# Two one-column shifts on the Vector engine written as one two-column instruction, in a cross-attention and feed-forward kernel

## The reference

```python
x = x + xattn(layernorm(x), ctx, ctx, igate_w, igate_b, fgate_w, fgate_b, out_w)   # 8 heads of 64
x = x + ffn(layernorm(x), kernel, input_scale, kernel_scale, bias)                 # fp8-rounded 512x512 product

def layernorm(x, eps=1e-05):
    m, v = mean(x), var(x)                 # over the 512 values of a row
    return (x - m) / sqrt(v + eps)
```

## Time and profile before

| What | us |
|---|---|
| median of 3 runs | 1698.84 |
| the runs | 1691.91, 1698.84, 1705.91 |
| the profiled execution, its own time | 1687.96 |
| its span, first to last instruction | 1686.2 |
| busy in it: PE, DVE, ACT, POOL | 1487.8, 1491.5, 1319.7, 1208.2 |

### The profile page before, as it was taken

One profiled execution on the slowest core, in us unless ns is written; L12 is line 12 of the kernel. 1 busy time (PEld: TensorE's weight loads), 2 busy tenths in 40 slices (PEclk: granted clock), 3 DMA queues, 4 the chain that ended last, 5 costly groups with the idle time before them and its releaser, 6 DMA issues.

```text
span 1686.2 us, 79011 instructions
## 1 busy us (share of the span) xinstructions
PE 1487.8 (88%) x31104; PEld 1046.6 (62%) x31104; DVE 1491.5 (88%) x4091; ACT 1319.7 (78%) x3206; POOL 1208.2 (72%) x1101
## 2 busy tenths in 40 slices
PE   1589998999999999899999899998999999999884
PEld 0366666666666666666666666666666666666662
DVE  5669999899989999989999899998999989998894
ACT  4568887888888888878888788887888878888662
POOL 2047777778777777867777777777777777777884
PEclk9789999999999999999999999999999999999996
DMA  5468888888888888877887878888788888887552
GB/s 182 135 197 250 261 257 246 247 250 257 260 242 267 253 257 245 265 239 241 261 251 257 251 238 253 264 254 257 245 250 260 263 251 245 270 253 233 192 170 82
DMA packets 138523, 402.61 MB, mean 239 GB/s; under 512 B 26216, under 2 KB 36456, under 8 KB 138152
## 3 DMA queue, kind: packets, MB, share of 16 engines
q1 hardware_dynamic: 138152, 397.52, 77.4%
HBM read 325.23 MB, written 72.22 MB: 236 GB/s over the span
## 4 chain that ended last, share of the span: by engine, by line
PE 31%; DVE 28%; DMA 19%; issue 13%; ACT 6%; POOL 3%; DVEq 1%; SPq 0%; ACTq 0%; POOLq 0%
DMA o_sb<-in_x 10%; PE work L555 7%; DMA out<-o_sb 5%; DVE o_sb L1076 5%; PE y L594 5%; DVE bn L1036 5%; DVE dec L982 4%; PE qk L523 4%; PE turn L451 4%; DMA x_sb<-in_x 3%; DVE bn L958 2%; PE turn L462 2%; POOL x L1234 2%; DVE carry L989 2%; DVE bn_h L1019 2%
## 5 line engine op out<-in xcount | busy, mean ns | idle before, releaser
L1216 POOL TENSOR_TENSOR x<-x,h_r 128x512 f32<-128x512 f32 x256 | 294.8, 1152 | 131.4 <-DVE x L1028 91.3
L1229 POOL TENSOR_TENSOR x<-x,w_out 128x512 f32<-128x512 f32 x256 | 358.1, 1399 | 17.7
L1234 POOL TENSOR_TENSOR x<-x,o_sb 128x512 f32<-128x512 f32 x256 | 321.4, 1277 | 52.9 <-DMA o_sb<-in_x 52.3
L555 PEld LDWEIGHTS work<-c_first,dec 128*64 128x64 f32 x4096 | 259.4, 138 | 93.6 <-issue 92.5
L555 PE MATMUL work<-c_first,dec 128*64 128x65 f32 x4096 | 291.1, 224 | 20.4 <-DVE carry L989 16.8
L555 PE MATMUL work<-c_sb,dec 128*64 128x65 f32 x4096 | 294.0, 225 | 0.0
L523 PE MATMUL qk<-qT,kT 64*64 64x128 f32 (+1 forms) x8192 | 238.5, 251 | 59.9 <-DVE dec L982 44.2
L594 PE MATMUL y<-w_ffn,zq 128*128 128x512 bf16 x1024 | 268.4, 385 | 2.2 <-issue 2.2
L523 PEld LDWEIGHTS qk<-qT,kT 64*64 64x64 f32 x8192 | 200.6, 134 | 100.4 <-issue 76.0
L555 PEld LDWEIGHTS work<-c_sb,dec 128*64 128x64 f32 x4096 | 259.2, 138 | 0.2 <-issue 0.2
L674 ACT ACTIVATE dec<-arg 128x384 f32<-128x384 f32 x512 | 243.0, 475 | 7.3 <-PE arg L505 6.1
(11 more groups left out here) (113 smaller groups left out, 3229.0 us busy)
## 6 DMA issues: line engine op xcount, KB each, us to landing
c_sb<-in_ctx SPq DMA_DIRECT2D x128, 520.0 KB, 7.2
x_sb<-in_x SPq DMA_DIRECT2D x128, 512.0 KB, 5.5
kT<-in_keys SPq DMA_DIRECT2D x128, 512.0 KB, 7.2
o_sb<-in_x SPq DMA_DIRECT2D x128, 512.0 KB, 5.2
out<-o_sb SPq DMA_DIRECT2D x128, 512.0 KB, 3.0
c_first<-in_ctx SPq DMA_DIRECT2D x256, 130.0 KB, 5.9
arg_queries<-query_parts SPq DMA_DIRECT2D x128, 144.0 KB
arg_keys<-key_parts SPq DMA_DIRECT2D x128, 12.0 KB
```

Of the source, the lines that this page charges most:

```text
L555: last = mm(work_ps[rows, u, c * W:(c + 1) * W], heads_dec[:, slot * Q:(slot + 1) * Q], src, start=True, stop=True)
L1216: pl.tensor_tensor(h, h, h_r[:, t * NH:(t + 1) * NH].unsqueeze(2).broadcast_to([P, NH, DH]), ALU.mult).then_inc(h_normed[t].sem, 1)
L1229: pl.tensor_tensor(h, h, w_out[:, :], ALU.mult).then_inc(h_scaled[t].sem, 1)
L1234: pl.tensor_tensor(x1[:, b.k % 2, t, :], x1[:, b.k % 2, t, :], o_sb[:, b.k % 2, t, :], ALU.add).then_inc(x1_set[t].sem, 1)
```

## The change

In `norm_scale` and in `mix_scale` the loop over the two tiles goes. It issued one tensor_scalar on one column each: the tensor input was the mean (mv, [128, 1]), the per-partition scalar operand was r ([128, 1]), and the second scalar the constant -1. In its place stands one scalar_tensor_tensor on two columns: (mv * -1.0) * r, with mv's two means (a stride of two elements) as first tensor and r's two columns as second tensor. The waits, the semaphore that is raised, and the place in DVE's order stay. Both tensors lie in SBUF.

```diff
@@ norm_scale
                 dve.wait_ge(*x_rstd.of(b))
                 if b.follows(2):
                     dve.wait_ge(*q_normed.of(b - 2))
-                for t in range(T):
-                    done = ts(nb1[:, b.k % 2, t:t + 1], mv1[:, b.k % 2, t, 0:1], r1[:, b.k % 2, t:t + 1], -1.0, ALU.mult, ALU.mult)
-                done.then_inc(x_shift.sem, 1)
+                stt(nb1[:, b.k % 2, :], mv1[:, b.k % 2, :, 0], -1.0, r1[:, b.k % 2, :], ALU.mult, ALU.mult).then_inc(x_shift.sem, 1)
@@ mix_scale
                 dve.wait_ge(*m_rstd.of(b))
                 if b.follows(1):
                     dve.wait_ge(*z_set.of(b - 1))
-                for t in range(T):
-                    done = ts(nb2[:, t:t + 1], mv2[:, t, 0:1], r2[:, t:t + 1], -1.0, ALU.mult, ALU.mult)
-                done.then_inc(m_shift.sem, 1)
+                stt(nb2[:, :], mv2[:, :, 0], -1.0, r2[:, :], ALU.mult, ALU.mult).then_inc(m_shift.sem, 1)
```

## The result

Measured: 1743.43 us median (1732.75 to 1753.44, 4 runs) against 1697.12 us of the kernel before with one more run, a ratio of 1.0267, 95% interval 1.0187 to 1.0346. The forecast was 1741 us. All ratios leave out executions over 1.5% above the fastest of their kernel; there is one, the profiled execution of e3 (1745.07 us).

What follows compares the result with a forecast made beforehand. No engine alone bounds it, but the fixed-order DVE is on the path for long stretches. Four slots' terms sum to 1.25 us, times 31 = 39, plus 3 of spill: 1698.84 + 42 = 1741 us, range 1698 to 1795.

Steps and rivals of the forecast that it cites:

- The mechanism, and that it makes the kernel slower: A DVE instruction with two SBUF tensors waits for POOL's already started instruction; slower by over 1%, chance 0.78.
- rival (a): POOL also wins the narrow races; the third slot's L975 turns from -0.16 to +0.94 us; 1779 us, chance 0.33.
- Who wins at 0.04 to 0.06 us: L975 starting this closely behind POOL's instruction in second to fourth slots: DVE taken to win, -0.16 us each.
- The won case that I read: L1028 starting 0.01 us after POOL's L1216 took 0.68 us while POOL waited; read as DVE winning there.
- I count the first and third slots in full: DVE delays count fully in these slots, without idle time; second and fourth swallow up to about 1.2 us each.
- forecast +0.51: First slot: L975 starts 0.46 us after L1229 and is held 0.67 us, less 0.16 saved.
- forecast 0.74, and 1.84 with the lost race: Third slot: L1053's hold behind L1197 gives +0.90 us; L975's race gives -0.16 if won, +0.94 if lost.
- L1053 behind L1216 in the fourth slot: Starts 0.09 us late; if POOL wins, held 0.82 us and L1028 thrown back some 1.3, mostly taken by slack.
- 0.24 us a pair against 0.08 us: In norm_scale and mix_scale, each fused pair gives back 0.16 us of DVE time; 41 us over 128 slots at most.
- Rival (b): The two-column instruction is not held, being small or its second operand short; 13 us faster, 1686 us, chance 0.12.
- Rival (c): Holds occur, but stretches paced by loads and PE swallow most; +10 us, 1709 us, chance 0.10.

Runs made afterwards that it cites:

- e3: Changed kernel with norm_scale's two means first copied to PSUM (from batch 9 on): 1730.65 us, 1.0323 of the kernel before.
- e2: Kernel before with only norm_scale as one scalar_tensor_tensor, mix_scale as the old pair: 1702.34 us, 1.0181 of the kernel before.
- e9: Kernel before with norm_scale alone fused, its means copied to PSUM (from batch 9 on): 1686.61 us, 1.0002 of the kernel before.
- e8: The changed kernel measured again, unaltered: 1751.19 us, 1.0404 of the kernel before.
- e5: Changed kernel with the means of both norm_scale (from batch 9 on) and mix_scale copied to PSUM first: 1707.69 us, 1.0114 of the kernel before.
- e4: Changed kernel with norm_scale moved one place earlier, ahead of the 0.08 us normaliser: 1754.29 us, 1.0471 of the kernel before.
- e1: Kernel before with only mix_scale as one scalar_tensor_tensor, norm_scale as the old pair: 1724.11 us, 1.0322 of the kernel before.
- e12: Kernel before with only mix_scale fused, and issued behind L989 instead of ahead of it: 1722.06 us, 1.0188 of the kernel before.
- e11: Kernel before with only norm_scale fused, issued earlier where POOL idles, and x_rstds ahead of keep_heads on ScalarE: 1697.49 us, 1.0057 of the kernel before.
- e6: Changed kernel with ScalarE's two 1/std instructions exchanged, the second normalisation's first: 1737.96 us, 1.0289 of the kernel before.

## Why the prediction was right or wrong

- **The mechanism, and that it makes the kernel slower**: right. The hold is shown by e3, where the memory of one operand decides it, and its cost in time by e2 beside e9 (1.0181 against 1.0002) and e8 beside e5 (1.0404 against 1.0114). Removing one hold of two did not give its time back in e3, which I had not foreseen. The rule of the Trainium skill on the shared port pair ("SBUF — State Buffer", section "SBUF: two separate sides"), that whichever engine starts first has it for its whole instruction, agrees with the traces, down to instructions of 0.13 us, wherever the DVE starts ahead of POOL or 0.07 us or more behind it; between these, both outcomes occur. The Trainium skill's advice to minimise the count of DVE operations ("VectorE: DVE Perf Modes", section "Rules for kernel authors"; the same table row warns against fusing for performance) brought nothing here: 256 instructions fewer, and 3% slower.
- **The time, 1741 us**: measured 1743. The agreement is luck; two steps were off in opposite directions. What happened is rival (a), and its own sum said 1779.
- **Who wins at 0.04 to 0.06 us** ("I take for the DVE at 0.04 to 0.06"; I had called it the weakest step): wrong. POOL wins 71 of 73, in the second to fourth slots: rival (a). The won case that I read, L1028 0.01 us behind, is near the edge: mix_scale loses at 0.01 (e3) and 0.03 (e4), L1028 at 0.04 (e5).
- **The price of rival (a), 1779 us**: too high, and with it the step "I count the first and third slots in full". In a cycle with hardly any idle time the single terms hold. The timeline of the changed kernel, where slots begin (answers to the earlier trace rows):

```profile
459.28 0.66 DVE L1026 TENSOR_TENSOR x<-g_sb,bn_h 128x512 f32<-128x512 f32 x1
...
472.31 0.66 DVE L1026 TENSOR_TENSOR x<-g_sb,bn_h 128x512 f32<-128x512 f32 x1
...
484.41 0.66 DVE L1026 TENSOR_TENSOR x<-g_sb,bn_h 128x512 f32<-128x512 f32 x1
...
496.92 0.66 DVE L1026 TENSOR_TENSOR x<-g_sb,bn_h 128x512 f32<-128x512 f32 x1
```

  The first slot lasts 13.03 us (from 12.54, forecast +0.51), the third 12.51 (from 10.81, +1.70; forecast 0.74, and 1.84 with the lost race). But 10.81 us was not what a third slot lasts. Over the middle 25 cycles the four kinds lasted 12.8, 12.1, 11.6 and 12.9 us on average before, with 0.4, 1.0, 0.9 and 1.5 us of idle time, and 13.4, 12.3, 12.6 and 13.0 after. The third slots grew by 0.9 us on average, not 1.7: only 7 of the 25 had lasted 10.8 us before, the others up to 13.3. I had taken one cycle of the trace for all.
- **L1053 behind L1216 in the fourth slot** ("the slot's slack takes most of it"): the race is lost as feared, but only 12 times, against 24 in e1 and 39 in e3, where norm_scale isn't held; with its hold mix_scale mostly comes ahead of L1216.
- **Terms that were left out of the sum**: the other engines' waits. I followed the late instruction only down the DVE's own order. ACT's wait for the second shift was 2.0 us before and is 26.8 us after, and e12 shows that such lateness, at 102.4 us, can cost 1.9%. ACT's wait for L1008, behind norm_scale, went from 7.6 to 78.1 us; what this one costs no run separates.
- **0.24 us a pair against 0.08 us**: right as far as seen. After an L1050 at 473.05 that is not held, L987 starts at 473.10, even sooner. The saving is nowhere in the time: e11, with norm_scale's share of it and without norm_scale's holds, is at 1.0057.
- **Rival (b)**: excluded by the 1220 ns. **Rival (c)**: the idle time did swallow 65 of 116 us, more than half of the added busy time, but what was left is 3%.

## What to carry to other kernels

Before fusing short DVE instructions, count tensor operands in SBUF: a pair with one tensor and a per-partition scalar each passes beside POOL in 0.33 us, one instruction with two SBUF tensors can wait for a whole POOL instruction. Look up in the timeline what POOL executes when it starts, and treat an offset of up to 0.06 us as undecided: in these runs both outcomes occur there. A hold shows as duration and never as a wait, so compare min/median/max of a line; and price it by who waits for its result on other engines, not only by what follows it on its own.

## What the runs showed of the hardware that was not expected

Who is held is decided by hundredths of a microsecond between starts, and not by the start times alone: mix_scale level with POOL or ahead wins, 0.03 us late it waits 0.9 us (e1, e4); norm_scale 0.04 to 0.06 us late loses 194 times and wins 15 (the changed kernel, e2, e6); and L1028 won at 0.01 30 times of 30 before and lost at 0.04 6 times of 6 in e5, but won there once each in e9 and e11. So delays of 0.03 us move instructions of 0.7 us to 1.5 us. The effects of two edits need not add: 1.032 and 1.018 alone, 1.027 and 1.040 together in two measurements, of which the second, up to 1.050, doesn't exclude the sum.
